# Three order edits in a two-layer attention and expert kernel: a context exponential, a root, and two tiles' normalized rows

## What is computed

```python
x = x + linear_attention(layernorm(x), ctx)     # "first attention": exp of q, exp of k
x = x + ffn_low_rank(layernorm(x))              # "second norm" in tensor names: norm 1 here
x = x + grouped_attention(layernorm(x), ctx)    # norm 2; 16 query heads, 4 key heads, softmax
x = x + experts_top4(layernorm(x)) + shared_expert(layernorm(x))   # norm 3; 16 experts
```

## Time and profile before

| | us |
|---|---|
| median of 3 runs | 690.94 |
| lowest, highest | 690.10, 691.38 |
| span of the profiled execution | 691.6 |

### The profile page before, as it was taken

The page is one execution under the profiler, slowest core; times in us unless marked ns, Lnnn a source line. Parts: engine busy times, 40 slices in busy tenths (PEclk is TensorE's granted clock), DMA queues, the critical chain, the costliest instruction groups (busy, mean ns, idle before and its releaser), DMA issues.

```text
span 691.6 us, 9803 instructions
## 1 busy us (share of the span) xinstructions
PE 668.3 (97%) x2424; PEld 398.3 (58%) x2425; DVE 336.1 (49%) x867; ACT 219.6 (32%) x626; POOL 175.1 (25%) x226
## 2 busy tenths in 40 slices
PE   9999999999999999999999989999999999999991
PEld 7555444456777767777776666574444444444440
DVE  3995224533334546687685767455233333333330
ACT  4574522213344433554446353220111111111110
POOL 2365100001000000014404223365123332333332
PEclk9999999999999999999999999999999999999997
DMA  9999999231400200001112005213777657868544
GB/s 339 408 421 420 422 421 398 93 108 63 151 1 0 92 1 1 0 3 60 62 52 102 35 28 189 116 78 106 260 191 148 140 99 188 194 147 223 94 60 57
DMA packets 60403, 103.18 MB, mean 149 GB/s; under 512 B 7200, under 2 KB 32544, under 8 KB 59712
## 3 DMA queue, kind: packets, MB, share of 16 engines
q1 hardware_dynamic: 30320, 73.48, 28.5%
q0 software_dynamic: 8816, 18.00, 12.8%
q10 hardware_dynamic: 21232, 11.28, 5.7%
HBM read 46.60 MB, written 56.26 MB: 149 GB/s over the span
## 4 chain that ended last, share of the span: by engine, by line
PE 84%; DVE 5%; DMA 3%; issue 2%; another core or an unknown queue 2%; ACT 1%; SPq 1%; POOL 0%; POOLq 0%; DVEq 0%; ACTq 0%
PE ps L1271 50%; PE ps L1460 12%; PE ps L1445 4%; PE ps L1429 4%; PE ps L1257 3%; PE ps L1376 3%; PE ps L1377 3%; PE ps L1386 3%; DMA r<-in_ctx 2%; DMA out<-rq,sidx 1%; PE ps L1398 1%; DVE st L983 1%; DVE qsum L1018 1%; DVE rq L1015 1%
## 5 line engine op out<-in xcount | busy, mean ns | idle before, releaser
L1271 PE MATMUL ps<-kv,rq 128*128 x432 | 192.7, 594 | 3.1 <-DVE rq L965 1.7
L1271 PE MATMUL ps<-zT,r 128*128 128x256 f32 (+1 forms) x552 | 132.5, 395 | 0.1
L1271 PEld LDWEIGHTS ps<-kv,rq 128*128 128x128 f32 x432 | 78.8, 190 | 90.5 <-issue 90.2
L1271 PEld LDWEIGHTS ps<-zT,r 128*128 128x128 f32 x552 | 103.5, 190 | 23.6 <-issue 10.1
L1460 PE MATMUL ps<-r 128*128 128x512 f32 x192 | 85.1, 593 | 0.0
L652 POOL DMA_INDIRECT out<-rq,sidx x36 | 56.6, 1573 | 110.5 <-DMA out<-rq,sidx 81.8
L579 POOL TENSOR_SCALAR ve<-mv 128x1 f32<-128x1 f32 x32 | 7.2, 224 | 257.3 <-DVE mv L984 257.3
L1196 DVE TENSOR_TENSOR rq<-ps,rq 128x256 f32<-128x256 f32 x36 | 15.3, 425 | 100.0 <-ACT rq L835 96.6
L783 ACT ACTIVATE r<-ps,snm 128x128 f32<-128x128 f32 x128 | 45.2, 365 | 54.8 <-DVE snm L1100 50.3
L1460 PEld LDWEIGHTS ps<-r 128*128 128x128 f32 x192 | 35.2, 190 | 38.3 <-issue 38.3
L835 ACT ACTIVATE rq<-ps 128x256 f32<-128x256 f32 x36 | 13.8, 383 | 118.2 <-PE ps L1271 108.6
(11 more groups left out here) (181 smaller groups left out, 860.2 us busy)
## 6 DMA issues: line engine op xcount, KB each, us to landing
slot_rows<-rq SPq DMA_DIRECT2D x4, 8192.0 KB, 50.4
kv<-in_experts SPq DMA_DIRECT2D x54, 256.0 KB
rq<-slot_rows ACTq DMA_DIRECT2D x138, 64.0 KB
r<-in_Wq SPq DMA_DIRECT2D x1, 3072.0 KB, 18.0
r<-in_Wo SPq DMA_DIRECT2D x2, 1536.0 KB, 6.4
r<-in_ctx SPq DMA_DIRECT2D x8, 256.0 KB, 8.3
xr<-in_x SPq DMA_DIRECT2D x8, 256.0 KB, 8.5
second_norm_rows<-zrow SPq DMA_DIRECT2D x8, 256.0 KB, 2.2
```

What stands on the lines that cost most here:

```text
L1271: mm = pe.matmul(out, lhs(k), rhs(k), start=(k == 0), stop=(k == n - 1))
```

## The change

Three edits.

First, `a_prep j+3` goes ahead of `ln_z 1 j-2`, `ln_stat 1 j-1` and `a_stat j+4` in the loop of the first attention. It carries ScalarE's exponential of the context tile ahead of the norm rows (696 ahead of 714), and VectorE's small multiply (999) ahead of the norm shift and both statistics.

Second, in the table for tiles 5 to 7 `ln_z` goes from place 1 to place 0 of offset 8. This applies to tile 5 (n = 28) and tile 6 (n = 32); tile 7's place lies behind the loop's end, where its step is written out and unchanged. VectorE now makes these rows ahead of the output copies of `pv 26` and `pv 30`.

Third, the id scatter of tile 3 goes from behind tile 3's row scatters to behind the root of tile 5. GpSimd's order was rows 3, ids 3, root 5, rows 4, rows 5, root 6, ids 4; it becomes rows 3, root 5, ids 3, rows 4, rows 5, root 6, ids 4. The rest is the same.

```diff
@@ -305,14 +305,14 @@
             prog.append(unit())
+            if j + 3 < J:
+                prog.append(("a_prep", j + 3))
             if j >= 2:
                 prog.append(("ln_z", 1, j - 2))
             if j >= 1:
                 prog.append(("ln_stat", 1, j - 1))
             if j + 4 < J:
                 prog.append(("a_stat", j + 4))
-            if j + 3 < J:
-                prog.append(("a_prep", j + 3))
             if j >= 3:
                 prog.append(("ln_t", 1, j - 3))
@@ -366,7 +366,7 @@
-               ((6, 0, "op0"), (7, 0, "op1"), (7, 1, "ln_stat"), (8, 1, "ln_z"), (9, 2, "ln_t"), (9, 1, "gate"),
+               ((6, 0, "op0"), (7, 0, "op1"), (7, 1, "ln_stat"), (8, 0, "ln_z"), (9, 2, "ln_t"), (9, 1, "gate"),
                 (10, 1, "place"))]
@@ -597,7 +597,7 @@
                     root(J * step[1] + step[2])
-                    if step[1] == 3 and step[2] >= J - 2:
+                    if step[1] == 3 and step[2] >= J - 3:
                         place_ids(step[2] - 2)
@@ -618,7 +618,7 @@
-                    if j < J - 4:
+                    if j < J - 5:
                         place_ids(j)
```

## The result

| | before | after |
|---|---|---|
| median, us (20 runs each) | 690.42 | 693.50 |
| lowest, highest, us | 688.69, 694.76 | 689.27, 697.65 |
| span of the profiled execution, us | 691.6 | 693.3 |
| time of that execution, us | not given | 695.14 |

What follows compares the result with a forecast made beforehand. TensorE, busy 97% of the span, was taken as the bound. Profiled span 691.6 - 1.4 + 0 + 2.35 + 1.6 = 694.1; carried to the median, 690.94 + 2.55 = 693.5 us (chance 0.50), range 690.2 to 695.2.

Steps and rivals of the forecast that it cites:

- Edit 1: First attention: both TensorE waits for the context exponential go, gaining 0.62 + 0.80 = 1.42 us, taken as 1.4.
- Tile 5: Earlier root and rows only move TensorE's wait from the transposes to tile 4's gate; 0, ends -1.0 and +1.7 us.
- none of that moves: Before tile 4's gate: ScalarE's copies and exponentials, busy 1.92 and 1.97 of 2.00 us, keep their times, so gain 0.
- its end of -1.0 us: Ahead of tile 4's gate: ScalarE's 0.6 us copy waited 0.9 us for TensorE's late signal, which may not be late again.
- at full clock: Ahead of tile 4's gate: TensorE waits from about 407 to 409.6 us without a lower clock.
- The other end, +1.7 us: At tile 5: the slow end of the term taken as 0, set by the clock, 1.7 us.
- Tile 6: Rows wait for GpSimd's late root and hold up the copies; TensorE idles about 2.65 us at `pv 31`, cost 2.35 us.
- The clock: Behind the wait at `pv 31`: a fall to the lower level, 1.6 of 1.7 us paid; ends 0 and 1.7 us.
- Clock stays up: At tile 6: the same 2.65 us wait brings no lower clock; 691.9 us, chance 0.22.
- Scatters in time: At tile 6: GpSimd waits for no landing, root 1.9 us earlier, `pv 31` 0.9 us late; 690.4 us, chance 0.09.
- Root not late: At tile 6: the root is no longer late, only the first attention's gain stands; 689.5 us, chance 0.08.
- Gain of edit 1 lost: Another wait replaces those of the first attention, or the clock also falls on tile 4's gate; 694.9 to 695.2, chance 0.11.

Runs made afterwards that it cites:

- the change again: The whole unaltered change, timed and profiled once more against the kernel before on another chip; ratio 1.0024, interval 1.0001 to 1.0046.
- the part alone: Only tile 6's rows moved ahead of the output copies of `pv 30`, on the kernel before; ratio 1.0067, +4.7 us (3.1 to 6.3).

## Why the prediction was right, and where it was not

The time and the direction came as forecast: +2.55 us against +2.6 (1.0038) and +1.7 (1.0024). The mechanism that decides it, at tile 6, did too. But that the number fits so closely is partly luck: two gains were put too small, the clock's cost at tile 5 was left out, and these errors cancel. The median of 693.50 meets the forecast only because that of before was 0.5 us lower than the one the forecast started from.

**Edit 1: right, its size too small.** Predicted 1.42 us, the two waits as the profile lists them. Measured 1.80 us of TensorE's time over the two rounds, with the same 10.42 us in the eight other traces with this edit (without it 12.22 in before, 12.42 to 12.45 in four others), and 2.2 us in the times (-3.7 to -0.8, which can't tell the two sizes apart). A round of before lasts 44.01 - 38.02 = 5.99 and 50.24 - 44.01 = 6.23 us, one without a wait 5.21: the waits listed as 0.62 and 0.80 us cost 0.78 and 1.02. The step that failed is to take a listed wait for the time that is lost. The ends of matmuls are modelled, and the wait begins at that end: line 1312 is listed with 1.02 us, but in after the transposes start 0.87 us behind its start (46.92 to 47.79), so some 0.15 us of each wait are not listed. A round of the same work without a wait is the measure of the loss. That TensorE would meet no other wait up to 400 us held, and the gain is there at 400 us.

The Trainium skill (Perfetto Trace Analysis, "Tensor Engine Instruction (MATMUL, LD_WEIGHTS)") says that the profiler estimates the end of a TensorE instruction instead of observing it. The 0.16 and 0.22 us by which these two waits were listed too short are in line with that.

**Tile 5: wrong in its size.** Predicted 0, with -1.0 and +1.7 us as ends. Measured about -2.0 us without the clock's loss for both steps and -1.2 us for the scatters alone; by the traces TensorE reaches gate 4 1.2 and 1.1 us sooner. The step that failed first is "none of that moves": ScalarE's chain to the gate did move, since its first copy no longer waited for a late signal of TensorE. The prediction had named this, as its end of -1.0 us, and taken 0 without a reason from a row. The rest of the picture came as described: the root at 397.60, which is 400.05 on the clock of before (2.45 us of lead), the rows behind at 400.83 (403.28), the gate still behind ScalarE's copy, a wait of 1.87 us ahead of it. Only "a little over 2 us earlier" for the root was too little by the prediction's own sign of 400 to 401 us: it is 3.2 us.

The second step that failed is the wait "at full clock". The other end, +1.7 us, was real as well and larger: the wait now ends directly ahead of the gate, what stands behind is the full work of TensorE, and the lower clock there cost 3.3 us in after and 1.7 us in the change again, against nothing in the one profile of before. How often before itself pays there isn't known; the first edit alone did (1.6 us), so the times of before may hold some of it, and that would make the edits look better in the ratios than in the profiles.

**Tile 6: right.** Predicted: the row step ahead of the copies with a wait of 5 us or more, TensorE idle 2.65 us at `pv 31`, 2.35 us of it paid. Measured: waits of 5.62 us on VectorE, 2.17, 1.93 and 3.19 us on TensorE, and 2.5 us in the span without the loss for the part alone. From the product ahead of `pv 31` to gate 6 it cost 3.6 us in after and 3.3 in the change again, with the lower clock, and 2.9 us in the part alone without it; by the times 4.7 us (3.1 to 6.3), against 2.35 + 1.6 = 3.95 predicted. Moving tile 5's scatters behind the root took the whole of it away.

**The clock: right for the place that was named, for the most part.** The lower level came behind the wait of tile 6 in two profiles of the change (0.56 and 0.58, 0.59 and 0.56 in the windows, 1.7 us of full speed each), and not in the profile of tile 6's part alone, behind a wait of 3.19 us. Over the executions the change lost 1.4 to 2.5 us more than before; 1.6 was predicted, for this place alone, and tile 5's share is in it.

**The sum.** The two profiles of the change, each against that of before, show how TensorE's lead came and went (us; minus is late):

| TensorE at | after | change again |
|---|---|---|
| product ahead of tile 5's stretch, 398.25 in before | 2.51 | 2.17 |
| gate 4, 409.63 | 3.74 | 3.40 |
| transposes behind the projection, 417.56 | 0.41 | 1.72 |
| product ahead of `pv 31`, 431.85 | 0.41 | 1.72 |
| gate 6, 442.24 | -3.17 | -1.62 |

Of these leads 0.65 and 0.3 us are from the start and no edit's. The forecast had 1.4 us in the first row, the same in all rows to the fourth, and -2.55 in the last. So it is the term of 0 for tile 5 that was wrong most, by both a gain and a larger cost that it did not have.

By the ratios the parts give -2.2 - 1.8 + 4.7 = +0.7 us, and the change measured +1.7 and +2.6. Some 1 to 2 us of the change are thus not told by its parts one by one. The intervals of the three single ratios are each about 1.4 us wide to either side, so it can be their error; what it is stays open.

**The rivals.** Clock stays up: no, by the windows of both profiles of the change; in that of tile 6's part alone it did stay up. Scatters in time: no, two of the row scatters still waited 1.79 and 1.17 us for a landing; the landing took 4.6 to 7.9 us from the issue in after (line 618, 421 to 433 us), longer than the prediction's estimate of 2.6 us. Root not late: no, VectorE waited 5.62 us. Gain of edit 1 lost: no. The clock a second time, on the gate of tile 4: yes, in both profiles of the change. It stood in the case of 0.11 with up to 695.2 us, and its price was offset by the larger gains.

**One choice of base.** The profiled execution of before was put at 0.65 us above the median, by its span. In after, time less span is 1.84 us; if that held for before, its execution took some 693.4 us, 3 us above the median. The difference of the two profiles, 1.7 us, is therefore smaller than that of the medians.

## What to carry to other kernels

Before a step that waits is put ahead of one that does not, look up when the thing it waits for is ready, and what stands ahead of that on its own engine: the same move cost nothing at tile 5, where the root had been moved up too, and lost 4.7 us at tile 6, where tile 5's scatters stood ahead of the root. Before crediting such a move, take away its companion: nearly all of tile 5's gain was the scatters' place. Price a TensorE wait by the length of a round with it and one without it, not by the idle time listed. A wait of some 2 us is dearer ahead of a dense stretch than ahead of one that waits again, since the lower clock behind it falls on work: the same 1.7 us cost under 0.2 us on a stretch that waited and 1.6 to 1.7 us on the projection.

## What the hardware showed that was not expected

TensorE's signals arrived 1.0 to 2.5 us behind the modelled end of the work, on ScalarE and VectorE alike, for a stretch of some 2 us (401.9 to 404.4 us in before). They did so in each of the four traces with eight indirect DMAs in a row on GpSimd there, 392.95 to 403.22 us in before; in the ten with the root between the fourth and the fifth, GpSimd pausing 1.93 us for it in after, they were prompt, though scatters ran from 398.67 us on beside the same work. So their mere presence isn't the cause. That the gate starts 1.1 us earlier behind its product without them says that time was really lost, and not only recorded late. What delays them is not shown.

The clock did not follow the length of a single wait. It stayed at full over waits of 1.72 us and once of 3.19 us, and fell behind 0.52 and 1.87 us that lay 1.1 us of work apart. Where it fell mattered more: in the nine profiles in which it fell behind gate 4, what was lost on the projection was paid to within 0.6 us.
